# Other table sizes, unit 11's short operations on VectorE, and a new order of all steps in a chunked-memory layer with routed experts

## What is computed

```python
out = retrieved @ Wo.T
out = out * rsqrt(mean(out * out) + EPS) * norm_g * (hidden @ gW.T + gb)
x = layernorm(x + out)
chosen = argmax(x @ gate_w.T)              # one of 8 experts per token
x = layernorm(x + (x + x @ expert_w[chosen].T))
```

## Time and profile before

| | us |
|---|---|
| median of 3 runs | 485.21 |
| lowest, highest | 483.51, 486.47 |
| the profiled execution | 488.3 |
| its span in the profile | 487.1 |
| busy TensorE, VectorE, ScalarE, POOL | 434.8, 393.4, 311.2, 269.9 |

### The profile page before, as it was taken

The page is one execution under the profiler, slowest core; times in us unless marked ns, Lnnn a source line. Parts: engine busy times, 40 slices in busy tenths (PEclk is TensorE's granted clock), DMA queues, the critical chain, the costliest instruction groups (busy, mean ns, idle before and its releaser), DMA issues.

```text
span 487.1 us, 11131 instructions
## 1 busy us (share of the span) xinstructions
PE 434.8 (89%) x3538; PEld 335.8 (69%) x3538; DVE 393.4 (81%) x1233; ACT 311.2 (64%) x791; POOL 269.9 (55%) x354
## 2 busy tenths in 40 slices
...
GB/s 235 169 141 57 132 130 58 153 113 97 174 102 157 107 179 94 186 100 174 110 155 177 107 182 126 133 148 255 143 177 175 174 187 249 177 199 239 188 101 50
DMA packets 61353, 73.20 MB, mean 150 GB/s; under 512 B 17293, under 2 KB 48206, under 8 KB 61296
## 3 DMA queue, kind: packets, MB, share of 16 engines
...
...
## 4 chain that ended last, share of the span: by engine, by line
PE 56%; ACT 17%; DVE 13%; issue 5%; POOL 4%; DMA 3%; SPq 1%; DVEq 0%; POOLq 0%; ACTq 0%
PE bank L636 9%; PE bank L539 9%; PE bank L1379 5%; PE bank L560 4%; PE bank L998 3%; ACT junk L1008 2%; DVE kq_in L589 2%; ACT os L1421 2%; PE bank L1076 2%; PE bank L1089 2%; PE both L953 2%; PE bank L829 2%; ACT rows L1068 2%; PE both L893 2%; POOL out L1426 1%
## 5 line engine op out<-in xcount | busy, mean ns | idle before, releaser
L1426 POOL DMA_INDIRECT out<-os,xs_token x71 | 70.3, 990 | 35.1 <-issue 11.0
L1146 POOL DMA_INDIRECT sorted_rows<-rows,index x64 | 74.6, 1166 | 24.7 <-issue 12.8
L589 DVE SCALAR_TENSOR_TENSOR kq_in<-shared,conv_w,kq_in 128x256 f32<-128x256 f32 x144 | 61.4, 479 | 10.3 <-ACT kq_in L580 10.1
L636 PE MATMUL bank<-front 128*128 128x256 f32 x256 | 63.1, 393 | 0.9 <-DVE bias_g L333 0.9
L1379 PE MATMUL bank<-shared,front 128*128 x228 | 57.6, 398 | 6.7 <-ACT front L1353 3.0
L539 PE MATMUL bank<-front 128*64 128x256 f32 x512 | 60.7, 388 | 0.3
L636 PEld LDWEIGHTS bank<-front 128*128 128x128 f32 x256 | 47.7, 195 | 9.5 <-issue 2.3
L1379 PEld LDWEIGHTS bank<-shared,front 128*128 128x128 f32 x228 | 42.8, 197 | 15.4 <-issue 10.1
L539 PEld LDWEIGHTS bank<-front 128*64 128x64 f32 x512 | 35.8, 139 | 20.6 <-issue 2.7
L1386 DVE BATCH_NORM_STATS2 st<-bank 128x6 f32<-128x256 f32 x57 | 21.7, 421 | 20.4 <-PE bank L1379 20.0
L1068 ACT ACTIVATE rows<-y,rstd 128x256 f32<-128x256 f32 x64 | 35.1, 592 | 4.2 <-POOL rstd L1061 3.8
...
## 6 DMA issues: line engine op xcount, KB each, us to landing
...
```

The lines of the kernel that those rows point to most:

```text
L589: dve.scalar_tensor_tensor(dst, raw[g][:, kind, :, tap:tap + P], conv_w[:, kind, tap:tap + 1], dst, ALU.mult, ALU.add))
L636: ins = pe.matmul(bank[:, (b % 2) * H:(b % 2 + 1) * H], xt[:, k, b * P:(b + 1) * P], w_g[:, k, :], start=k == 0, stop=k == KH - 1)
L1146: pool.indirect_dma_start(sorted_rows[:, :], bass.IndirectOffsetOnAxis(index[i3][:, b:b + 1], 0), R[:, b, :], None, bounds_check=NE * REGI ...
L1426: pool.indirect_dma_start(out[:, :], bass.IndirectOffsetOnAxis(xs_token[t % LOADS][:, i:i + 1], 0), os_[o][:, i, :], None, bounds_check=TO ...
```

## The change

Three constants and the whole string change. Table 0 is made after 11 units and not 12, with 36 tiles and not 40; the next after 13 (8 tiles) and 15 (8 tiles, was 4). So pairs 0 to 17 come from table 0 (were 0 to 19), 18 to 21 from the table of 13 units (were 20 to 23 from that of 14), 22 to 25 from the table of 15 units (were 24 and 25); the last table gives pairs 26 to 35 in both. Unit 11's short operations take the late form. The string has 2391 steps and not 2388: the late form has two steps more in the epilogue and one more in `learn`.

```diff
-TABLES = ((12, 40), (14, 8), (15, 4), (NC * G, NT - 52))
+TABLES = ((11, 36), (13, 8), (15, 8), (NC * G, NT - 52))
 WIDE_ON_DVE = 0
-SMALL_ON_DVE = 12
+SMALL_ON_DVE = 11
...
 ORDER = (
-    "p0p0p0p0p0p0p1p0p0p0p0p0p0p0p1p0p0p0p0p0p0p0p0p1p1p1p1p1p1s0p1p1p1g0p1p1p1p1p0p1p1p1p1p0p0p1p1p1l0s0p0p0p3s0p1l0l0p0p1p0"
+    "p1p0p0p0p0p0p0p0p0p0p0p0p0p0p0p0p0p0p0p2p0p1p0g0p0p1p1p1p1p1s0p1p1p1p1p1p1p1s0p0p1p1p1p1p1p0p1p0p1p1s0p0p1p0p0l0l0l0p1l0"
...
-    "ebeaseebleebpfleseebleleley0lfy0y0ebebpfy0lflfleededpfeblfpfpfeceaedececebebsfecpfpfececy0pfsflfecpfsflepfecsfy0lesfedy0"
+    "leseleeby0rdebleeaebleeay0lfleseebebpfpflfebsfy0lfpfy0ebpfrdpfpepfpfsfpfecleebedy0ececlfpfecedeclflfpfedededx0seleedsfle"
...
-    "edececx3sfx4edecx1x3reecedreedrfeceex4x2rfx0rfx2x2ecx2x1eeeex2x2eeeeedeex3x4edx3ecx2x2eex1x3x3x2x1x2rfedeex2x4eex2ededx0"
+    "sfedrex2x4lfecedlfrfx3x3x2reedy0x1x0x4edeceerfrfedx2ecx2x0x1rfedeeeex4x1x2x0eex2x4eeeeedx3x3eeeeeex2x2x1x4ecx0x4x1x2x2x2"
...
-    "x4efx2x2efx2x2x0z0x3x2x3x2efn0z0z0x1efx4x4efx2x3x2x4efx1x2x3x1z0x2z0x4x2efx2x3x1x0efefx0x4x2x2z0x4x4x1x4x2x2x1x2x2x2x2z0"
+    "x2efx2x4x2x4x2x4x0efz0efefx3z0z0z0x0x2x1z0x2efefx2x2x3x4x4efx1x2x1x2x1x4efx2x1x2x4x3x3x2x2x2efx4z0x2x3x3x2z0x2z0x0x4x4x4"
...
```

More of the change, by code:

```diff
@@ L1454 @@
[L1454 to L1465, removed]
@@ new lines @@
+    "s0l0l0p0l0s1l0s0s1s0l0p1s0l0l0l0p1l0s1s0l0l1l1s0s0s0p0p1s1p1s1p1p2s0l0p2p2p1l0p2p2p2s0p1p2s0p2s0l0p2l0l1p2p2p2l1p3p2p2p2"
+    "p2s1p2p2p2p2l1l1l1s2l1p1l0p2l1s0p2p2l0s1s1s1s2l1l1l1l1r0l1l1s1s1r0r0s1l2p2p3l1p3p3l1p3p2r0l2s1s2l1r0l1p3p3p3p3s2l2l1r0l2"
+    "s1p3s2r0s1p3p3p3p3p3l2p3p3p3s1p3p3s2p4p2r0r1p3p2l2r0l2e0r1p3s2r1p2l2p3p3l2s2e0e0s3p3l2p3p3s3l2e0e0p3l2l2e0l2e0l2r1r0e0e0"
+    "p3l3s2l2p5s2s2s3l3r0p4p4p4l2l2s3s3s2r1s2p3l3p4e0s3e0p4r0e0p4s2l3r1e0p4p4p4e0p3r1s3l3p4p4p4p4p4l3p4p4p4p4e0p4r1p4p4r1e0e0"
@@ new lines @@
+    "e0l3e0l3r1l3r0e0e0p3l3e0e0s2l2l3s2e0r1l2l3s3l3l3s4e0p4p4r0e0s4s3r2r2e0r2l3l4e0e0l4l3l3p4l3r2e1p4l4s4s3s4e0s3e0s4s3l3s3l3"
+    "r2e1e1e1e0r2e1e1p5r2e1s4p5p5l4p5s3p5e0l4p5p5r1p5l4p5e1s3l4l4l4p5e0p5p5r2p5p5p5l4p5p5e0p5p5e1l4l4p5p5p4s3l4r2s4r1e1s5p5l4"
+    "p4r3p5e1e2r3s5r1e2e1p6e2e1r3s4p5p5r3e2e1l5l4e1l4r2s5s4s4p5s4l5l4e2p6e2s4e0s5p5e1e1s5p4p5p5r3p6s4e2p6r2l4e1p6p6s5e1e1p8r3"
+    "e2e0l5p6p6e0r3r2p6l5p5p6p6p6s5p6p6s4p6p5p6l5p6l5e2e0p6p6p6e1p6e1r3e1e1l5l5l4l5l4e2s6r3r2e1l5e2e1e0l5e1e1r4par4e2p6r2l5e1"
@@ new lines @@
+    "s5e2l5e2e0e3s4r4s4p6e1p6e3l5p7e1e2s5e3p9l5l5e3p6p6e1r4e3s6s6r3l5l5e2l6e2l6r3e2e3p7e3s5l5e3e2r4r4e2s6e2l6r3s6e3s5p7e2s5l5"
+    "e2e2p7e2e2p7l6p7r4s5e1l6s5s6l6l6e1p7p7p7s6p7s6l6e1p7p7p7p7e1e2r4p7e2e2p7r4p7p7p7e3p7e1p6l6r5p7p7e3p7p6e4r5p7e4e3p6r3r5s5"
+    "e2p7e1s5e1r3p7e4e3e4p7l6r5e3l6l6r4l6e3l6s7p7s6s7e4e4e4p7r4l7s6s7e4p8s6s7s6e3e3l6e3e1e3e3p7p8p8p8l7s7p8s6e4e1s6p8e2p8r5l6"
+    "s6l6e2r5l6s7p8p7p7e2e2p8e3l7r5s7e3p8l7l7e2l7p8p8e4e2l6p8l6e4p8p8e2p8p8p8p8l7e2p8r5e3e4l7r5l7r5e3r4e2e3l7s6p8e3e4r6p8e3e3"
```

48 lines of the change are left out of this document (24 added, 24 removed).

## The result

The changed kernel took 499.0 us (median of 4 runs, 496.08 to 503.28); the kernel before, run beside it, 485.84. The ratio is 1.0294, 95% interval 1.0184 to 1.0405: slower by 2.9%, by 1.8% at the lower end of the interval. The profiled execution took 500.8 us, span 499.5.

A forecast was written before the change was run, and what follows sets the result against it. TensorE was taken to set the pace up to pair 4, POOL's scatters from there. Terms -0.4 - 1.0 - 1.6 - 1.0 - 0.7 + 1.5 gave -3.2 us, so 482 us by the median, range 473 to 490.5.

The forecast's parts named there:

- POOL's queue sets the end: From pair 4's first scatter on, POOL is full: 75 scatters and 2 loads, 98.5 us, plus its holes.
- the early tables: Making table 0 after 11 units instead of 12 was valued at 0 (bounds -2.1 us to 0).
- The test set for it: The tables part is wrong if pair 4's first scatter moves over 4 us while TensorE's earlier idle time stays.
- The five places: Five priced spots: gate weights, router scores, 300 to 366 us, pair 4's output, the hole at 451 us.
- Place 1: Gate weights: VectorE makes them before unit 1's taps, shortening TensorE's 0.9 us wait; -0.4 us (-0.9 to 0).
- place 2: Router scores: more steps between cut TensorE's 2.9 us of waits for turned rows; -1.0 us (-2.9 to 0).
- Place 3: 300 to 366 us: TensorE's waits for unit 11's rows, softplus sum and e_t; -1.6 us for all (-4.6 to 0).
- Place 4: Pair 4's output: ScalarE's two scalings now stand ahead of pair 5's square root; -1.0 us (-1.2 to 0).
- Place 5: POOL's hole at 451 us: pair 23's load now stands behind SyncE's padding stores; -0.7 us (-2.0 to +1.3).
- Unit 11's operations: Short operations leave POOL for VectorE (1.5 us) and ScalarE (3.2 us, two table loads); +1.5 us (0 to +4.7).
- ScalarE's switches: Rival, 0.15: unit 11's loads and roots delay unit 15's copies and unit 12's rows on ScalarE; slower, 492 us.
- A hole where pair 22 or 23 comes: Sign that the forecast is right: POOL waits 1 to 2 us at pair 22 or 23.

The follow-up runs named there:

- e7: Before's first 1,922 steps (to pair 4's first scatter), then the changed kernel's sequence, with before's tables and unit 11 on POOL; ratio to before 1.0020.
- e6: Before's first 1,770 steps (to pair 0's transposes), then the changed kernel's sequence, with tables of 12, 13, 15 and 16 units, unit 11 on POOL; ratio 1.0105.
- e10: As e6, but before's sequence is kept longer, up to unit 13's second output product; ratio to before 1.0054.
- e17: e6 with one step moved: unit 14's first row statistics placed behind unit 13's index; ratio to before 1.0062.
- e2: The changed kernel's tables and order, with unit 11's short operations back on POOL; ratio to before 1.0223.
- e5: The changed kernel's first 1,499 steps (to about 305 us), then before's order, with before's tables and unit 11 on POOL; ratio to before 1.0093.
- e9: e5 with the next unit's hidden states' load issued ahead of SyncE's wait for the gate's transfers, from unit 4 on; ratio to before 0.9994.
- e15: Before with the late form for unit 11's output side alone, its gradient side left on POOL; ratio to before 1.0072.
- e18: The changed kernel with early hidden-state loads, unit 11 back on POOL, and unit 14's first statistics behind unit 13's index; ratio to before 1.0138.
- e11: Before with 95 small products that nothing reads, ahead of pair 24's transposes alone; ratio to before 0.9974.
- e16: Before with the late form for unit 11's gradient side alone, its output side left as before; ratio to before 1.0013.
- e1: Before's tables and order, with only unit 11's short operations in the late form (three steps put in); ratio to before 1.0061.

## Why the prediction was wrong

**What holds: POOL's queue sets the end.** 98.5 us of work were foreseen from pair 4's first scatter to the end of the last, which is 97.5 from start to start; the twenty kernels have 96.9 to 98.4, and holes of 0 to 7.0 us beside it (before 2.0, after 3.7). e7 shows it from the other side: a new sequence behind that scatter costs 0.2% by its median, 0.6% at most by its interval. Because the end is pair 4's start plus this work and its holes, what was lost before pair 4 came through.

**What may hold: the early tables.** Nothing was expected of them, and nothing shows that they gave or cost anything. Pair 0's load waits for unit 15's projection, not for a table. ScalarE's last copy of it and the load's issue on SyncE, in before and in after:

```profile
350.07 0.18 ACT L665 ACTIVATE theta<-bank 128x8 f32<-128x8 f32 x1 [2.34 <-PE bank L661]
...
352.64 6.53 SPq L1336 DMA_DIRECT2D front<-sorted_rows  x8
```

```profile
355.73 0.18 ACT L665 ACTIVATE theta<-bank 128x8 f32<-128x8 f32 x1 [1.27 <-PE bank L661]
...
356.90 0.98 SPq L1336 DMA_DIRECT2D front<-sorted_rows  x2
```

The test set for it (pair 4 moving by over 4 us while TensorE's idle time stays) did not separate the cases, as pair 4 moved for other reasons. No run has the tables alone, and e6, e10 and e17 have new tables beside a new sequence, so a cost of theirs is not excluded.

**The step that failed** is the one sentence in the sum: "The rest of the sequence is shuffled too; what new waits that makes I can't price by rows, and take 0, with 4 us either way". Five places were priced, -4.7 us in all, and the many others taken as 0 on balance. They cost some 10 us (13.2 in all, less 3.5 of unit 11; e2, without it, 2.2%). The bound of 4 us came from TensorE's 4.9 us of idle time in 60 to 300 us, but that is what a new order can win there, not what it can lose. Two of the unpriced places were shown: the hidden states' load (e5 to e9, 1.0%), and statistics that wait for a transfer ahead of an index (e6 to e17, 0.4% by the medians). The first was in reach: the load stands on SyncE behind the gate's transfers, its latency and the step that needs it can be read in the trace, and the prediction reads SyncE's queue only around pair 24. A third cause, unit 11's roots (e15, 0.7%), was priced, too low. The rest, about half of the 2.9% by e18, was placed in e18's trace but not traced to a step by an experiment, and its cause stays open.

**The five places.** Place 1 was right in kind: TensorE's wait for the gate weights (0.9 us) no longer shows in after's waits. So was place 2: the waits for turned rows at the scores, 2.9 us before, are not in after's list from 60 to 300 us; -1.0 was too little. Neither gain was kept: TensorE's idle time in the first 60 us went from 8.1 to 9.1 us, and from 60 to 300 the four new waits for hidden states took 3.9. Place 3 was right on the three waits named (6.8 us became 2.6) and wrong in leaving out what would be late next, four other waits of 6.2 us. Place 4 was right at its step: pair 4's scalings follow unit 14's root by 1.5 us in after, where before has 2.6:

```profile
394.02 0.30 ACT L1012 ACTIVATE rms<-ssq,eps_rms 128x4 f32<-128x4 f32 x1
...
395.50 1.02 ACT L1421 ACTIVATE os<-bank,rs 128x256 f32<-128x256 f32 x2 [1.00 <-DVE rs L1409]
```

But the root itself came 12.9 us later than in before, and POOL's wait before pair 4 grew from 2.37 to 3.05 us. Place 5 was half right: the hole at 451 is gone, but the same kind of hole came before unit 15's scatter (2.07 us). e11 shows what the hole in before was worth, 0.3%, and that it could be had with one fill.

**Unit 11's operations** were put at +1.5 us with bounds 0 to +4.7, on the ground that VectorE's share counts and the loads don't. The size was too small, though within the bounds, and the reason wrong: e16, VectorE's short operations on the gradient side, is at 1.0013, and e15, the output side with the roots on ScalarE, at 1.0072, some 3.5 us. The rival "ScalarE's switches" had the right queue and a price of 4.7 to 6.6 us, but not the place. It named unit 12's rows and unit 15's copies; in e15's trace it was unit 10's rows, by the loads and the first root (0.9 us), and unit 11's own, by a root and a reciprocal (0.8 us). So the loads did count. The count of 25 loads was right (e1 and e15 have 25 too, e16 has 23), and each takes the 1.28 us of the earlier trace rows with the next operation 0.01 us behind it where nothing else holds that up. The Trainium skill, page "ScalarE: Activation LUTs", section "What ACT_TABLE_LOAD costs", has a drain of about 1.38 us beside it; no run here shows one.

**The other tests.** Scatters 1.28 us apart to the end: right. Pair 4's first scatter between 380 and 384: wrong, 396.86. Holes under 5 us after pair 4: right, 3.7. TensorE's waits at L1076 and L661 near 1 us: right, 1.10 and 1.20. A hole where pair 22 or 23 comes: wrong, it came ahead of unit 15's scatter.
